# Graph message passing on one core: third target buffer, scatter moved behind fold and queries, addition four groups back, last group in two halves

## What is computed

```python
w = silu(ef1 @ rad_W1 + rad_b1) @ rad_W2 + rad_b2
w = w + (silu(ef2 @ sph_W1 + sph_b1) @ sph_W2 + sph_b2)      # per edge, 128 wide
q = (x @ Wq)[dst]; k = (x @ Wk)[src]; v = (x @ Wv)[src]
alpha = (q * w * k).reshape(-1, 8, 16).sum(-1) / sqrt(16) * edge_weight[:, None]
out = segment_sum(alpha[..., None] * v, dst) / 16
y = layernorm(x + out)
```

## Time and profile before

| | us |
|---|---|
| median of 3 runs | 1971.99 (1971.89 to 1974.09) |
| profiled execution | 1972.41 |
| its span | 1970.7 |
| TensorE busy | 1729.7 |
| VectorE busy | 1569.1 |
| GpSimd busy | 1488.5 |
| ScalarE busy | 580.7 |
| mean granted TensorE clock | 0.937 |

### The profile page before, as it was taken

One profiled execution on the slowest core, in us unless ns is written; L12 is line 12 of the kernel. 1 busy time (PEld: TensorE's weight loads), 2 busy tenths in 40 slices (PEclk: granted clock), 3 DMA queues, 4 the chain that ended last, 5 costly groups with the idle time before them and its releaser, 6 DMA issues.

```text
span 1970.7 us, 56844 instructions
## 1 busy us (share of the span) xinstructions
PE 1729.7 (88%) x14511; PEld 1261.0 (64%) x14511; DVE 1569.1 (80%) x4324; ACT 580.7 (29%) x1030; POOL 1488.5 (76%) x1569
## 2 busy tenths in 40 slices
PE   8789889898989988888988898989888888898887
PEld 7566666666666656666666666666666666666665
DVE  5578888787877878877978877878778788788787
ACT  5322232222322322322332222232222222222223
POOL 7777777777777777777777777777777777777777
PEclk9899899998988999998999998998899899889898
DMA  9866656666656556556556555656656565656554
GB/s 338 259 172 172 165 163 174 163 169 168 168 161 171 165 166 171 163 165 173 164 164 174 161 167 164 173 164 173 164 165 167 160 175 162 165 163 166 172 156 116
DMA packets 191076, 339.02 MB, mean 172 GB/s; under 512 B 82989, under 2 KB 101022, under 8 KB 190750
## 3 DMA queue, kind: packets, MB, share of 16 engines
q0 software_dynamic: 74240, 202.21, 36.5%
q1 hardware_dynamic: 107440, 126.14, 22.2%
q10 hardware_dynamic: 9070, 7.02, 1.6%
HBM read 320.25 MB, written 14.95 MB: 170 GB/s over the span
## 4 chain that ended last, share of the span: by engine, by line
PE 22%; DMA 21%; SPq 20%; POOL 18%; issue 13%; DVE 5%; DVEq 1%; ACT 0%; ACTq 0%
POOL kvt L655 18%; DMA dbt<-dst 14%; SPq L582 13%; PE bank L693 10%; DMA kvt<-kvtab,srcS 4%; PE bank L670 3%; SPq L576 3%; SPq L591 2%; PE bank L708 2%; DMA out<-partn 2%; PE bank L695 2%; PE bank L732 2%; DVE t L979 1%; PE bank L301 1%; PE bank L683 1%
## 5 line engine op out<-in xcount | busy, mean ns | idle before, releaser
L655 POOL DMA_INDIRECT kvt<-kvtab,srcS x1528 | 1450.9, 950 | 466.3 <-issue 456.5
L770 ACT ACTIVATE hs<-bank,B 128x512 f32<-128x512 f32 x806 | 510.5, 685 | 1350.3 <-issue 804.6
L693 PE MATMUL bank<-W2r,hs 128*128 128x128 f32 x3224 | 499.5, 302 | 8.3 <-ACT hs L770 8.3
L693 PEld LDWEIGHTS bank<-W2r,hs 128*128 128x128 f32 x3224 | 424.2, 205 | 86.6 <-issue 75.3
L693 PE MATMUL bank<-W2s,hs 128*128 128x128 f32 x3224 | 456.7, 288 | 0.0
L966 DVE TENSOR_TENSOR t<-bank,kvt 128x512 f32<-128x512 f32 (+1 forms) x396 | 265.4, 670 | 207.9 <-PE bank L695 131.9
L693 PEld LDWEIGHTS bank<-W2s,hs 128*128 128x128 f32 x3224 | 424.8, 205 | 0.0
L708 PE MATMUL bank<-msg,oh 128*32 128x128 f32 x3216 | 179.0, 294 | 164.0 <-DVE accT L913 160.6
L708 PEld LDWEIGHTS bank<-msg,oh 128*32 128x32 f32 x3216 | 70.6, 110 | 355.7 <-issue 300.4
L981 DVE TENSOR_REDUCE bank<-t 128x32 f32<-128x512 f32 x403 | 280.1, 695 | 13.9
L979 DVE TENSOR_TENSOR t<-bank,t 128x512 f32<-128x512 f32 x403 | 274.2, 680 | 4.2 <-PE bank L683 3.2
(11 more groups left out here) (106 smaller groups left out, 702.7 us busy)
## 6 DMA issues: line engine op xcount, KB each, us to landing
kvA<-kvtab ACTq DMA_DIRECT2D x3968, 1.0 KB
eft<-in_ef SPq DMA_DIRECT2D x102, 512.0 KB, 7.7
kvS<-kvtab SPq DMA_DIRECT2D x3200, 1.0 KB
dbt<-dst SPq DMA_DIRECT2D x102, 384.0 KB, 6.1
kvt<-kvtab,srcS POOLq DMA_INDIRECT x1528
qwt<-qtab SPq DMA_DIRECT2D x403, 24.0 KB
kvtab<-kvt SPq DMA_DIRECT2D x24, 256.0 KB, 7.9
qtab<-qx SPq DMA_DIRECT2D x12, 384.0 KB, 6.3
```

Source lines behind the costliest of these rows:

```text
L655: pool.indirect_dma_start(kvt[:, (g - HX) % KS, t, :], None, kvtab, bass.IndirectOffsetOnAxis(ap=srcS[:, g * TG + t:g * TG + t + 1], axis= ...
L693: pe.matmul(WB[g % 2][:, t * D:(t + 1) * D], hs[:, g % HS, j, t * 128:(t + 1) * 128], w2[:, :], start=(j == 0 and t == 0), stop=False, ski ...
L770: act.activation(hs[:, g % HS, j, :], HB[i % 4][:, :], ACT.Silu, bias=B1[:, j:j + 1]).then_inc(m_si, 1)
```

## The change

What it does:

- The targets get three buffers in place of two and are requested at groups 0, 4, 8, ... for the next four, in place of 2 groups later.
- First products have one buffer in place of two, messages three in place of four; a wait for the scatter is written ahead of the message where VectorE makes no copy itself. The prologue's temporaries move into the feature buffers, with a wait each for VectorE and SyncE.
- TensorE's order in a group becomes second layer, fold of g - 4, queries, scatter of g - 3, first layer. The addition, the copy, and the steps of the norm inside the loop come one group later.
- The last group gets `half`, called for tiles 0 and 1 and again for tiles 2 and 3, with a semaphore of its own (`m_kvz`) for the last two gathers.

```diff
@@ row_tiles @@
-        if g >= n_groups:
+        if g >= n_groups - 1:
@@ gnn_program @@
-    KS, ES, DS, QS, HS, MS, OS, WS = 15, 3, 2, 6, 4, 4, 3, 6
+    KS, ES, DS, QS, HS, MS, OS, WS = 15, 3, 3, 6, 4, 3, 3, 6
+    def landed(g):
+        return TG // 2 if g == NE - 1 else gathered(g)
-        t1 = sb("t1", [128, 2, TG, D], f32)
+        t1 = sb("t1", [128, TG, D], f32)
@@ prologue @@
-            xgT = psb("xgT", [128, 2, G], f32)
+            xgT = eft[:, 2, :, :]
+            qrest = eft[:, 1, :, :].rearrange("p k (a f) -> p k a f", f=D)
+            dve.wait_ge(s_win, 4)
-            act.wait_ge(s_hp, 2 * HX)
+            for eng in (act, sp):
+                eng.wait_ge(s_hp, 2 * HX)
@@ SyncE @@
-                if b < NQP and (g == 0 or g % 4 == 2 and b >= 2):
+                if g % 4 == 0 and b < NQP:
@@ GpSimd @@
-                for t in range(gathered(g)):
+                for t in range(landed(g)):
...
+            for t in range(TG // 2, TG):
+                col = (NE - 1) * TG + t
+                pool.indirect_dma_start(
+                    kvt[:, (NE - 1 - HX) % KS, t, :], None, kvtab,
+                    bass.IndirectOffsetOnAxis(ap=srcS[:, col:col + 1], axis=0),
+                ).then_inc(m_kvz, 16)
@@ TensorE @@
             for g in range(NE):
-                if 3 <= g < NE - 2:
-                    scat(g - 3)
-                l2(g)
-                if g >= NE - 2:
-                    scat(g - 3)
-                    gq(g)
-                if g >= 3:
-                    fold_tiles(g - 3)
-                if g < NE - 2:
-                    gq(g)
+                l2(g)
+                if g >= 4:
+                    fold_tiles(g - 4)
+                gq(g)
+                if g >= 3:
+                    scat(g - 3)
                 if g % 2 == 0 and g // 2 + 1 < NP:
                     l1(g // 2 + 1)
             scat(NE - 3)
+            fold_tiles(NE - 4)
@@ VectorE @@
-            for g in range(NE):
+            for g in range(NE - 1):
-                if 3 <= g < NE - 2:
-                    accumulate(g - 3)
+                if 4 <= g < NE - 2:
+                    accumulate(g - 4)
-                if 0 <= g - 2 < LC:
-                    collect(g - 2)
+                if 0 <= g - 3 < LC:
+                    collect(g - 3)
                 if g >= NE - 2:
-                    accumulate(g - 3)
+                    accumulate(g - 4)
+                if g - MS >= LC:
+                    dve.wait_ge(m_sc, g - MS + 1)
...
+            g = NE - 1
+            dve.wait_ge(m_kv[(g - HX) % KS], 16 * sum(landed(i) for i in range(HX + (g - HX) % KS, g + 1, KS)))
+            dve.wait_ge(m_w, g + 1)
+            accumulate(g - 4)
+            half(g, 0, TG // 2, 0).then_inc(m_half, 1)
+            accumulate(NE - 4)
             accumulate(NE - 3)
+            dve.wait_ge(m_kvz, 16 * (TG - TG // 2))
+            half(g, TG // 2, TG, 4).then_inc(m_msg, 1)
             accumulate(NE - 2)
```

More of the change, by code:

```diff
@@ L175, in gnn_program @@
         m_kv = [sem(f"m_kv{i}") for i in range(KS)]
+        m_kvz = sem("m_kvz")
         m_ef = [sem(f"m_ef{i}") for i in range(ES)]
@@ L622, in gnn_program @@
                 sp_rows(g)
-                if g - 17 in use_n:
-                    store(use_n[g - 17])
+                if g - 18 in use_n:
+                    store(use_n[g - 18])
             q, b = max(range(0, NQP, ES)), max(range(0, NQP, DS))
@@ L629, in gnn_program @@
             destinations(0, m_db[0])
-            for g in range(NE, NE + 17):
-                if g - 17 in use_n:
-                    store(use_n[g - 17])
+            for g in range(NE, NE + 18):
+                if g - 18 in use_n:
+                    store(use_n[g - 18])
             sp.wait_ge(m_ef[0], features_landed(q) + 16)
@@ L813, in late_collect @@
                     act.activation(part[:, g % 2, :], strips(g)[:, 0:D], ACT.Copy).then_inc(m_part, 1)
-            for g in range(NE + 12):
+            for g in range(NE + 13):
                 if g < NE:
                     silu(g)
-                if g - 5 in use_n and use_n[g - 5] not in late:
-                    square(use_n[g - 5])
-                if g - 12 in use_n and use_n[g - 12] not in late:
-                    scale(use_n[g - 12])
+                if g - 6 in use_n and use_n[g - 6] not in late:
+                    square(use_n[g - 6])
+                if g - 13 in use_n and use_n[g - 13] not in late:
+                    scale(use_n[g - 13])
                 if g < NE:
@@ L939, in kv_parts @@
                 return ((0, TG, rows),)
-            def halves(g):
-                for a, b, kv in kv_parts(g):
-                    for c in range(a, b, TG // 2):
-                        e = min(b, c + TG // 2)
-                        yield c, e, kv[:, c - a:e - a, :]
             def alpha(g):
@@ L965, in gnn_program @@
                 for a, b, kv in kv_parts(g):
-                    m = dve.tensor_tensor(t1[:, s, a:b, :], tiles(WB[s][:, :])[:, a:b, :], kv[:, :, 0:D], ALU.mult)
+                    m = dve.tensor_tensor(t1[:, a:b, :], tiles(WB[s][:, :])[:, a:b, :], kv[:, :, 0:D], ALU.mult)
                 m.then_inc(m_t1, 1)
-                if 3 <= g < NE - 2:
-                    accumulate(g - 3)
+                if 4 <= g < NE - 2:
+                    accumulate(g - 4)
                 if g + 2 < NE:
                     window_T(g + 2)
-                if g - 5 in use_n:
-                    first_guess(use_n[g - 5])
+                if g - 6 in use_n:
+                    first_guess(use_n[g - 6])
                 for i in range(3):
-                    if g - 6 - i in use_n:
-                        refine(use_n[g - 6 - i], i)
+                    if g - 7 - i in use_n:
+                        refine(use_n[g - 7 - i], i)
                 dve.wait_ge(m_t1, g + 1)
                 dve.wait_ge(m_q, g + 1)
-                dve.tensor_tensor(t2[:, :, :], tiles(QB[:, :]), t1[:, s, :, :], ALU.mult).then_inc(m_t2, 1)
+                dve.tensor_tensor(t2[:, :, :], tiles(QB[:, :]), t1[:, :, :], ALU.mult).then_inc(m_t2, 1)
                 dve.wait_ge(m_t2, g + 1)
@@ L997, in gnn_program @@
                 dve.wait_ge(m_al, g + 1)
-                for a, b, kv in (halves(g) if g == NE - 1 else kv_parts(g)):
+                if g - MS >= LC:
+                    dve.wait_ge(m_sc, g - MS + 1)
+                for a, b, kv in kv_parts(g):
                     m = dve.tensor_tensor(msg[:, g % MS, a:b, :].rearrange("p t (h d) -> p t h d", h=H),
@@ L1034, in gnn_program @@
             for i in range(KS):
-                pool.wait_ge(m_kv[i], 16 * sum(gathered(g) for g in range(HX + i, NE, KS)))
-            pool.dma_reset(range(m_kv[0].num, m_kv[-1].num + 1))
+                pool.wait_ge(m_kv[i], 16 * sum(landed(g) for g in range(HX + i, NE, KS)))
+            pool.wait_ge(m_kvz, 16 * (TG - TG // 2))
+            pool.dma_reset(range(m_kv[0].num, m_kvz.num + 1))
             nc.all_engine_barrier(sems_to_clear=sems)
```

38 lines of the change are left out of this document (29 added, 9 removed).

## The result

| | before | changed |
|---|---|---|
| median, us (6 runs each) | 1973.35 (1971.89 to 1974.38) | 1992.51 (1989.17 to 1993.89) |
| ratio | 1 | 1.0097, 95% interval 1.0087 to 1.0107 |
| span of the profiled execution | 1970.7 | 1991.7 |
| mean granted TensorE clock | 0.937 | 0.963 |

The changed kernel is slower by 19 us. The forecast of 1974.3 and its range to 1984.0 are wrong; what came is close to rival (2), priced at 1989.

The account below looks back on a forecast made before the run. GpSimd's back-to-back gathers were taken as the bound, hiding the loop's changes (0); the tail's +2.3 us on a 1970.7 span gave 1973.0, 1974.7 profiled, 1974.3 us as a median, range 1970.0 to 1984.

Parts of the forecast that it names:

- rival (2): Loop of TensorE and VectorE no longer catches up with the gathers: mean above 4.69 us, 1989 us at 4.73; chance 0.15.
- GpSimd never stops: Gathers on GpSimd: 1528 stay, back to back at 1.255 us a step; effect of the change 0.
- The start: First groups needing a buffer back: the 0.88 us margin rather grows, effect 0; bound perhaps 1 us of stall.
- Target waits gone: VectorE's 78.0 us of target waits should go with the third buffer and earlier requests; -36.1 us in groups 7 to 235.
- Even groups at 4.83: TensorE's scatter ahead of the first layer: even groups take 4.83 us, 0.53 more; hidden by GpSimd.
- At a mean of 4.69: Pace deciding whether VectorE wins back 57.4 us in 380 groups; the forecast 4.61 us a group lay 0.08 below.
- The tail: Last groups: second layer stands behind the scatter, last scatter ends later, +2.3 us; bounds -1.7 and +5 (lower clock).
- The halves: Last group split in two: 2.0 us each, half A to 1963.8, half B from 1964.4 to 1966.4.
- rival (1): Last group: the halving pays, -1.7 us, 1970.3, no change; chance 0.12.
- the disagreement that it noted: VectorE's 512-wide step: 0.69 us by the profile row, 0.59 by the skill's table; the prediction kept to the row.

Follow-up runs that it names:

- the repetition: The changed kernel run again, unedited, against the kernel before on the same chip: ratio 1.0102 (1.0085 to 1.0119).
- the variant with both old orders: The changed kernel with the first layer back ahead of the scatter and targets requested at 2, three target buffers kept: ratio 1.0064 (1.0043 to 1.0085).

## Why the prediction was wrong

**GpSimd never stops: right**, to 2 us. 1528 gathers, back to back but for 9.0 us of waits, one of them real. **The start** was called "rather grows" and shrank, from 0.88 to 0.27 us, the 1.41 us idle being near the stall that the text had given as a bound. Product 7 came 2.4 us later than before.

**Target waits gone: right, and worth nothing.** This is the step that failed. It took VectorE's waits for targets as a cost of two buffers and subtracted them (41 groups, -36.1 us), while "SyncE's query and row transfers queue behind it" was costed at nothing. SyncE had 13.8 us of slack in 1078 us, of which 2.2 for a target buffer, so a wait for its transfers could only move to another of them: target waits 78.0 to 0, idle ahead of the queries 15.0 to 90.6. With eight rows SyncE sets the pace of the changed kernel (4.738, and 4.597 with seven). That it set the 4.634 of the kernel before too follows from its missing slack and was not tested in these surroundings. One view, the queue's own waits, would have told it. In groups 7 to 235 the forecast had 4.61, the runs 4.738 and 4.719. That the pace got worse than 4.634 and not just stayed is SyncE's 21.1 us, 34.3 more for row issues and 11.8 less for target issues.

**Even groups at 4.83: right as a spacing** (median at full clock 4.88, and 4.31 with the order undone and targets at 1), **wrong as a cost**: in the surroundings of the result, undoing the order gains nothing that can be told (1.0064 against 1.0081, where nothing else differs; 1.0126 against 1.0102, where the targets moved too). Odd groups are at 3.99, forecast 3.75 from one group; in the kernel before, too, their median is 3.93.

**Rival (2): the time, and the deciding point.** "At a mean of 4.69" fits from both sides: at 4.691 product 401 is 3.4 us behind the last gather, at 4.597 it is 0.4, at 4.712 and more 9.6 to 18.7. 0.048 us above the point times 380 gives 18 us, measured 16.1. Its mechanism as the text gave it, the wait for the addition no longer covered, is not what did it: seven rows give 4.597 in the same order. That 1989 lies close to 1992.51 is luck as far as that mechanism goes. Its chance of 0.15 was too low for a point 0.08 us away from an estimate that rested on a removed wait.

**The tail: right in mechanism**, +2.3 forecast, 2.9 measured at full clock, and 4.5 in the repetition and with seven rows, where the last second layer fell into the lower clock; the text's bound for that was +5, and the lower clock came in eleven of the sixteen profiles with the late addition (+5.3 with targets at 1). The halves did not pay: rival (1) is refuted, for the last group's half A starts 5.75 us behind the product of 401, where the whole group started 4.22 behind it. The first product was forecast near 1961.8, that is, 5.7 behind 1956.14. The halves took 2.0 us each, as forecast; the 0.6 that the forecast lacks lies in the step between them (0.88 us from message to product, where it had 0.6), the last scatter (1.12 us behind the message, where it had 0.9) and the start. The 256-wide steps took 0.42 to 0.43 us, as the prediction's row had it. The 58 cycles that it took from the Trainium skill (VectorE: DVE Perf Modes, TRN2 errata) stand there for operands in SBUF, while each of these steps reads or writes a bank, so the disagreement that it noted is one of its own reading.

**Left open.** Which part of the change adds the blocked issues. With the targets' place undone they are 88 us instead of 108 and 104, about half of the excess over 73 and 69 (one profile); with the order undone too 91, with two target buffers too 83. The rest of the change, above all the addition four groups back with its three message buffers, remains in every variant that was run, and was not undone by itself. What in the transfers makes an issue block is not known either. No version was found that beats the kernel before.

## What to carry to other kernels

Before a buffer is priced against a wait for a transfer, look at the waits of the queue that asks for it: here a queue with 13 us of waits of its own in 1078 set the pace, and a buffer with an earlier request only moved the lateness to its next customer. Where one engine must catch up with another, turn the distance into a deciding rate first, and set the chances by the forecast's distance from it: here 0.08 us a group, and the forecast missed by 0.13. In an in-order engine, work that has nothing to do with a wait belongs ahead of it where that wait is on the path that ends last: in the last group the tail grew by 2.9 us, while in the loop the same kind of move cost nothing that could be told.

## What the runs showed of the hardware

Eight row transfers of 1 KB cost SyncE 2.59 us to ask for, and 5.07 us some microseconds behind a 384 KB transfer (7.28 at the worst in the changed kernel); the long batches lie behind 384 or 512 KB transfers, and behind those that ScalarE asked for as well. One more such row a group on ScalarE, which is busy for 29% of the span by the page, made the changed kernel 1.7% slower (1.0270 against 1.0097) although SyncE was relieved, and the variant with both old orders 1.6% (1.0226 against 1.0064): a share of busy time does not count the issues. After 1.92 us without matmuls TensorE ran the second layer in 3.68 us at a granted clock of 0.54 with seven SyncE rows, partly at the lower of its two levels (1.2 and 2.4 GHz), and in 2.05 us at 1.00 after the same 1.92 us with the eleventh row on ScalarE; after 1.97 us it took 2.05 us at 1.00 in one profile of the changed kernel and 3.26 us at 0.59 in the other. So the length of that pause alone does not decide it. After 0.48 us, in one profile, it stayed at 1.00.
